# Context attention of a two-layer decoder: softmax division moved behind the weighted values, row sums by head-mask matmuls, the end of a row quantization on GpSimd

## The reference

```python
q = query @ Wq + bq;  kv = context @ Wkv + bkv          # 16 heads, head width 8
scores = einsum('bhid,bhjd->bhij', q, k) * 8 ** -0.5
scores = where(mask, -inf, scores)
attn = softmax(scores, axis=-1)
out = einsum('bhij,bhjd->bhid', attn, v)                 # heads side by side: 128 columns
x = x + out @ Wout + bout

def fp4_quant_dequant(x):                                # blocks of 16 along the row
    scale = max(max(abs(xb)) / 6, 1e-12)
    return grid(abs(xb / scale)) * sign(xb) * scale
gate = fp4_linear(layernorm(x), w_gate);  y = fp4_linear(layernorm(x), w_up)
x = x + fp4_linear(silu(gate) * y, w_down)
```

## Time and profile before

| | us |
|---|---|
| median of 3 runs (1272.89 to 1273.5) | 1272.97 |
| the profiled execution, its own time | 1272.73 |
| its span in the trace | 1270.8 |
| PE busy | 1128.9 (89%) |
| DVE busy | 901.9 (71%) |
| ACT busy | 879.7 (69%) |
| POOL busy | 627.9 (49%) |

### The profile page before, as it was taken

The page is one execution under the profiler, slowest core; times in us unless marked ns, Lnnn a source line. Parts: engine busy times, 40 slices in busy tenths (PEclk is TensorE's granted clock), DMA queues, the critical chain, the costliest instruction groups (busy, mean ns, idle before and its releaser), DMA issues.

```text
span 1270.8 us, 17038 instructions
## 1 busy us (share of the span) xinstructions
PE 1128.9 (89%) x6055; PEld 589.1 (46%) x6055; DVE 901.9 (71%) x1756; ACT 879.7 (69%) x1150; POOL 627.9 (49%) x463
## 2 busy tenths in 40 slices
PE   4899999999999999987888898799997999985765
PEld 2444444444444444432333332277775676653444
DVE  5766667766767677657888978546746786878885
ACT  2799999999989998992666767755564676733311
POOL 2577777777767777595455545013330300054232
PEclk9999999999999999996889989999998999997877
DMA  7200000000000000020000000000001000000000
GB/s 178 66 1 2 1 1 1 1 1 1 1 1 1 1 1 1 1 68 1 18 1 1 1 1 1 2 1 1 1 1 63 1 1 1 1 1 0 1 9 25
DMA packets 25631, 14.47 MB, mean 11 GB/s; under 512 B 14558, under 2 KB 24396, under 8 KB 25420
## 3 DMA queue, kind: packets, MB, share of 16 engines
q1 hardware_dynamic: 25548, 13.39, 3.7%
HBM read 12.34 MB, written 1.05 MB: 11 GB/s over the span
## 4 chain that ended last, share of the span: by engine, by line
PE 31%; POOL 31%; issue 20%; DVE 16%; ACT 1%; DMA 0%; POOLq 0%; SPq 0%; ACTq 0%; DVEq 0%
DVE ARENA L1159 6%; POOL ARENA L2711 6%; POOL ARENA L2709 6%; POOL ARENA L2705 6%; PE PS L1030 5%; POOL WQ L2722 3%; POOL ARENA L2735 3%; PE PS L900 3%; PE PS L1414 2%; PE PS L1004 2%; PE PS L832 2%; PE PS L1438 2%; PE PS L848 2%; PE PS L1405 2%; POOL WQ L2724 2%
## 5 line engine op out<-in xcount | busy, mean ns | idle before, releaser
L2565 DVE TENSOR_SCALAR ARENA<-PS,ARENA 128x512 f32<-128x512 f32 x256 | 174.5, 744 | 66.7 <-PE PS L2199 66.3
L1159 DVE TENSOR_REDUCE ARENA<-PS 128x1 f32<-128x512 f32 x256 | 160.9, 683 | 28.2 <-PE PS L848 27.7
L1075 ACT ACTIVATE ARENA<-PS 128x1024 f32<-128x1024 f32 x128 | 128.9, 1026 | 61.9 <-PE PS L886 61.6
L2378 ACT ACTIVATE ARENA<-ARENA 128x2048 f32<-128x2048 f32 x64 | 122.2, 1912 | 60.6 <-DVE ARENA L2565 60.1
L2199 PE MATMUL PS<-ARENA 64*128 64x512 f32 x512 | 129.0, 623 | 0.0
L2385 ACT ACTIVATE ARENA<-ARENA,consts_sb 128x2048 f32<-128x2048 f32 x64 | 124.6, 1994 | 0.4
L2209 PE MATMUL PS<-ARENA 128*64 128x512 f32 x512 | 118.7, 606 | 1.3 <-issue 1.3
L2391 ACT ACTIVATE ARENA<-ARENA 128x2048 f32<-128x2048 f32 x64 | 118.4, 1898 | 0.0
L2718 POOL TENSOR_SCALAR WQ<-ARENA,consts_sb 128x512 bf16<-128x512 f32 x32 | 22.3, 696 | 159.1 <-DVE ARENA L2541 159.1
L1340 POOL TENSOR_TENSOR ARENA<-ARENA 128x512 f32<-128x512 f32 x32 | 40.7, 1271 | 121.4 <-DVE ARENA L1298 120.9
L848 PE MATMUL PS<-ARENA 32*128 32x512 bf16 x256 | 74.0, 415 | 24.9 <-DVE ARENA L1159 19.8
(11 more groups left out here) (301 smaller groups left out, 2606.3 us busy)
## 6 DMA issues: line engine op xcount, KB each, us to landing
ARENA<-in_window_bias_dram SPq DMA_DIRECT2D x1, 1536.0 KB, 6.3
WKVG<-in_L_attn_W_in_dram SPq DMA_DIRECT2D x3, 448.0 KB, 5.6
X<-in_x_dram SPq DMA_DIRECT2D x4, 256.0 KB, 5.4
W<-in_L_ffn_w_dram SPq DMA_DIRECT2D x1, 1024.0 KB
out_dram<-X SPq DMA_DIRECT2D x4, 256.0 KB, 2.3
BV<-in_L_attn_b_in_dram SPq DMA_DIRECT2D x1, 512.0 KB, 6.7
Wout<-in_L_attn_W_out_dram SPq DMA_DIRECT2D x1, 512.0 KB, 4.7
WQ<-in_L_attn_wq_dram SPq DMA_DIRECT2D x1, 512.0 KB, 3.3
```

Source lines behind the costliest of these rows:

```text
L1075: act.activation(PT[m % PT_SLOTS], bank(("cP", m)), ACT.Exp, scale=0.5).then_inc(sem("c_exp"), 1)
L1159: dve.tensor_reduce(NMX[:, w % 2, t, h:h + 1], bank(("cS", n, j)), AX.X, ALU.max, negate=True).then_inc(sem("c_max"), 1)
L2378: act.activation(chunk(u, half), chunk(u, half), ACT.Sqrt).then_inc(sem("rooted"), 1)
L2565: dve.tensor_scalar(D[:, u % 2, kt, hd, :], bank(("S", u, c)), K2[:, u % 2, kt, hd:hd + 1], 1e-30, ALU.add, ALU.max).then_inc(sem("guarded ...
```

## The change

- The weights are no longer divided by their sum before they are transposed. sums and normalized go (DVE L1844 and L1845, POOL L1899, 16 times each), and the transposes wait for the exponential alone, one step earlier; ACT's copy turned also comes one step earlier.
- For each batch PE computes, behind the values (job eO), a second accumulation of four 128 x 512 matmuls of the same transposed weights with the head mask const("vhead") (job eZ): each output row holds the sum of its head. ACT inverts it as exp(-ln(sum)) (invert_sums), at t = 2 of the next batch, ahead of that step's exponential. DVE multiplies it with the values from PSUM into OTE (weighted, at the same step, ahead of quantize_y), in place of ACT's out_copy.
- project_out, turn_quantized and quantized_out move by a step or two; silu(0) stands behind invert_sums(3).
- quantize_y stops after seven of its nine instructions; the last two (a subtraction and the multiplication by the scales) are done by POOL, scaled_y, behind its subtraction of steps 11 and 15 (for batches 0 and 1), behind its stage E loop (batch 2), and behind step 2 of F (batch 3). hidden(1) and hidden(3) wait for them.
- SE has six buffers, not seven.

```diff
@@ tensor_e @@
                 for g in range(4):
                     mm = pe.matmul(o, VX[b][:, g, :], PTE[:, b % 2, g, :], start=g == 0, stop=g == 3)
                 done(mm, ("eO", b))
+                o = begin(("eZ", b))
+                heads = const("vhead").rearrange("p (g c) -> p g c", g=4)
+                for g in range(4):
+                    mm = pe.matmul(o, heads[:, g, :], PTE[:, b % 2, g, :], start=g == 0, stop=g == 3)
+                done(mm, ("eZ", b))
...
-            for s in range(STEPS + 2):
+            for s in range(STEPS + 1):
                 d_tail(s)
                 for n in scores_at(s):
                     scores(n)
-                if s < 2:
+                if s < 1:
                     continue
-                n = s - 2
+                n = s - 1
                 b, t = divmod(n, QT)
-                pe.wait_ge(sem("e_p"), n + 1)
+                pe.wait_ge(sem("e_exp"), n + 1)
...
                 if t == 0 and b:
                     values(b - 1)
-                if t == 1 and b:
+                if t == 2 and b:
                     project_out(b - 1)
-                if t == 0 and b >= 2:
+                if t == 3 and b >= 2:
                     turn_quantized(b - 2)
@@ scalar_e @@
-            def out_copy(b):
-                full(act, ("eO", b))
-                act.copy(OTE[:, b % 2], bank(("eO", b))).then_inc(sem("e_o"), 1)
-
-            for n in range(STEPS + 3):
+            def invert_sums(b):
+                full(act, ("eZ", b))
+                if b:
+                    act.wait_ge(sem("e_o"), b)
+                act.activation(ISUM, bank(("eZ", b)), ACT.Ln).then_inc(sem("e_sum"), 1)
+                act.wait_ge(sem("e_sum"), b + 1)
+                act.activation(ISUM, ISUM, ACT.Exp, scale=-1.0).then_inc(sem("e_isum"), 1)
+
+            for n in range(STEPS + 2):
                 b, t = divmod(n, QT)
                 d_tail(n)
                 if t == 1 and b >= 2:
                     rstd(5, b - 2)
+                if t == 2 and 1 <= b < B:
+                    invert_sums(b - 1)
                 if n < STEPS:
                     act.wait_ge(sem("e_shift"), n + 1)
-                    act.activation(SE[n % 7], SE[n % 7], ACT.Exp).then_inc(sem("e_exp"), 1)
-                if n == STEPS + 2:
-                    silu(act, 0)
-                if n >= 3:
-                    turned(n - 3)
-                if t == 3 and 1 <= b < B:
-                    out_copy(b - 1)
-                if t == 3 and b >= 2:
-                    quantized_out(act, b - 2)
-            out_copy(B - 1)
+                    act.activation(SE[n % 6], SE[n % 6], ACT.Exp).then_inc(sem("e_exp"), 1)
+                if n >= 2:
+                    turned(n - 2)
+                if t == 1 and b >= 3:
+                    quantized_out(act, b - 3)
+            invert_sums(B - 1)
+            silu(act, 0)
             quantized_out(act, B - 2)
@@ vector_e @@
-            def sums(n):
-                dve.wait_ge(sem("e_exp"), n + 1)
-                if n >= 3:
-                    dve.wait_ge(sem("e_p"), n - 2)
-                link(dve.tensor_reduce(SUE[:, n % 3], SE[n % 7], AX.X, ALU.add))
-                dve.reciprocal(RCE[:, n % 3], SUE[:, n % 3]).then_inc(sem("e_rc"), 1)
+            def weighted(b):
+                full(dve, ("eO", b))
+                dve.wait_ge(sem("e_isum"), b + 1)
+                if b >= 2:
+                    dve.wait_ge(sem("x_new"), 4 * B + b - 1)
+                dve.tensor_tensor(OTE[:, b % 2], ISUM, bank(("eO", b)), ALU.mult).then_inc(sem("e_o"), 1)
 
             for n in range(STEPS + 2):
                 b, t = divmod(n, QT)
                 if n < STEPS:
                     shift(n)
-                if n >= 2:
-                    sums(n - 2)
                 d_tail(n)
+                if t == 2 and 1 <= b < B:
+                    weighted(b - 1)
                 if b >= 2 and t == 0:
...
                 if b >= 2 and t == 2:
                     quantize_y(dve, link, b - 2)
+            weighted(B - 1)
             quantize_y(dve, link, B - 2)
             hidden(dve, link, 0, None)
@@ quantize_y, pool_e, hidden @@
-            quantize(dve, link, X_SCRATCH[1], P, Y[:, b].rearrange("p t d -> p (t d)"), S, YQ[:, b % 2].rearrange("p t d -> p (t d)"), "f_yq", last)
+            quantize(dve, link, X_SCRATCH[1], P, Y[:, b].rearrange("p t d -> p (t d)"), S, None, "y_added", last)
+
+        def scaled_y(pool, b):
+            scratch = X_SCRATCH[1]
+            rows = scratch[3][:, 0:S]
+            by = lambda t: t.rearrange("p (k i) -> p k i", i=BLK)
+            pool.wait_ge(sem("y_added"), b + 1)
+            pool.tensor_tensor(rows, rows, scratch[2][:, 0:S], ALU.subtract).then_inc(sem("y_rounded"), 1)
+            pool.wait_ge(sem("y_rounded"), b + 1)
+            if b >= 2:
+                full(pool, ("fX", b - 2))
+            scales = scratch[0][:, 1, 0:S // BLK].unsqueeze(2).to_broadcast([P, S // BLK, BLK])
+            pool.tensor_tensor(by(YQ[:, b % 2].rearrange("p t d -> p (t d)")), by(rows), scales, ALU.mult
+                               ).then_inc(sem("f_yq"), 1)
...
+                if n in (11, 15):
+                    scaled_y(pool, n // 4 - 2)
+            scaled_y(pool, B - 2)
             for n in range(STEPSF):
...
+                if n == 2:
+                    scaled_y(pool, B - 1)
...
+            if n in (1, 3):
+                dve.wait_ge(sem("f_yq"), B - 1 + n // 2)
```

More of the change, by code:

```diff
@@ L467, in d_tail, with values @@
         return []
+    def values(b, *pool):
+        return [(("eO", b), 1, [("e_o", b + 1)], *pool), (("eZ", b), 1, [("e_sum", b + 1)], *pool)]
     jobs = scores(0, "E3") + scores(1, "E3")
-    for s in range(steps + 2):
+    for s in range(steps + 1):
         jobs += d_tail(s)
@@ L473, in stage_e_jobs @@
             jobs += scores(n, pool_at(s))
-        if s >= 2:
-            b, t = divmod(s - 2, QT)
-            jobs += [(("eT", s - 2), 1, [("e_pt", s - 1)], pool_at(s))]
+        if s >= 1:
+            b, t = divmod(s - 1, QT)
+            jobs += [(("eT", s - 1), 1, [("e_pt", s)], pool_at(s))]
             if t == 0 and b:
-                jobs += [(("eO", b - 1), 1, [("e_o", b)], pool_at(s))]
-            if t == 1 and b:
+                jobs += values(b - 1, pool_at(s))
+            if t == 2 and b:
                 jobs += [(("eX", b - 1), 1, [("x_new", 4 * B + b)], pool_at(s))]
-            if t == 0 and b >= 2:
+            if t == 3 and b >= 2:
                 jobs += [(("fX", b - 2), 1, [("f_x", b - 1)], pool_at(s))]
-    jobs += [job + ("E4",) for job in gate_and_up_jobs(0)]
-    return jobs + [(("eO", B - 1), 1, [("e_o", B)], "E2"), (("eX", B - 1), 1, [("x_new", 5 * B)], "E2"),
-                   (("fX", B - 2), 1, [("f_x", B - 1)], "E2")]
+    jobs += [job + ("E4",) for job in gate_and_up_jobs(0)] + values(B - 1, "E2")
+    return jobs + [(("eX", B - 1), 1, [("x_new", 5 * B)], "E2"), (("fX", B - 2), 1, [("f_x", B - 1)], "E2")]
 def gate_and_up_jobs(n):
@@ L756, in decoder_kernel @@
         PTE, _ = carve(0, [2, 4, S])
-        SE = [carve(k, [HX, CK])[0] for k in (5376, 5888, 6400, 6912, 7424, 7936, 30848)]
+        SE = [carve(k, [HX, CK])[0] for k in (5376, 5888, 6400, 6912, 7424, 7936)]
         OTE, _ = carve(15872, [2, S])
@@ L1829, in shift @@
                 full(dve, ("eS", n))
-                if n >= 7:
-                    full(dve, ("eT", n - 7))
+                if n >= 6:
+                    full(dve, ("eT", n - 6))
                 if n >= 2:
                     dve.wait_ge(sem("e_shift"), n - 1)
-                dve.scalar_tensor_tensor(out=SE[n % 7], in0=bank(("eS", n)).rearrange("p (h j) -> p h j", h=HX),
+                dve.scalar_tensor_tensor(out=SE[n % 6], in0=bank(("eS", n)).rearrange("p (h j) -> p h j", h=HX),
                                          scalar=SCALEX, in1=MB[:, b].unsqueeze(1).to_broadcast([P, HX, CK]),
@@ L1896, in pool_e @@
                 add_bias(b)
-            def normalized(n):
-                pool.wait_ge(sem("e_rc"), n + 1)
-                pool.tensor_tensor(SE[n % 7], SE[n % 7], RCE[:, n % 3].unsqueeze(2).to_broadcast([P, HX, CK]),
-                                   ALU.mult).then_inc(sem("e_p"), 1)
-            for n in range(STEPS + 2):
-                if n < STEPS:
-                    pool.wait_ge(sem("e_max"), n + 1)
-                    pool.tensor_tensor(SE[n % 7], SE[n % 7], NME[:, n % 2].unsqueeze(2).to_broadcast([P, HX, CK]),
-                                       ALU.subtract).then_inc(sem("e_shift"), 1)
-                if n >= 2:
-                    normalized(n - 2)
+            for n in range(STEPS):
+                pool.wait_ge(sem("e_max"), n + 1)
+                pool.tensor_tensor(SE[n % 6], SE[n % 6], NME[:, n % 2].unsqueeze(2).to_broadcast([P, HX, CK]),
+                                   ALU.subtract).then_inc(sem("e_shift"), 1)
                 if n == ETAIL["weigh_end"]:
```

8 lines of the change are left out of this document (3 added, 5 removed).

## The result

| | before | changed |
|---|---|---|
| median, us | 1272.93 (1271.22 to 1273.5, 4 runs) | 1296.46 (1294.57 to 1297.67, 4 runs) |
| ratio, 95% interval | | 1.0188 (1.0172 to 1.0203), all of it above 1 |
| span of the profiled execution | 1270.8 | 1292.8 |
| its own time | 1272.73 | 1294.57 |

What follows compares the result with a forecast made beforehand. DVE was taken to bound stage E, but DVE and ACT would stand in order behind each pair and inversion: 1272.73 + 21.6 (stage E) + 0.9 (stage F) = 1295.2 us, forecast 1295, range 1284 to 1304.

Steps and rivals of the forecast that it cites:

- What bounds: Stage E: DVE is the bound, so work taken from it (net 16.7 us) counts unless a wait takes its place.
- Batch 0: Stage E, first batch: pair eO, eZ starts at 1130.6 us; shift(8) at 1145.9 against 1140.49, 5.4 us lost.
- Batch 1: Stage E, second batch: pair takes 9.4 us, DVE stands 10.3 us before weighted, shift(11) at 1169.7 us.
- Batch 2: Stage E, third batch: pair takes 8.7 us, DVE stands 11.2 us, shift(15) ends at 1195.2 against 1180.6 us.
- Batch 3: End of stage E: full-clock pair of 7.1 us, DVE stands 12.5 us, hidden(0) at 1216.2 against 1194.60 us.
- a wait of 10 to 12 us ahead of each of the last three weighted: Sign expected in the new trace: DVE waits this long before weighted in batches 1 to 3, released by ACT's Exp.
- Stage F: After stage E: quantize_y(3) shortens by 1.33 us but hidden(3) waits 2.2 us for POOL; +0.9, bounds -1.3 to +2.
- Full clock in all pairs: Rival for stage E's pairs: slower, but PE keeps full clock since it has more to do; 1289.4 us, chance 10%.
- The clock not coming back within a pair: Rival for stage E's pairs: low clock throughout, adding 2.5, 3.2 and up to 4.8 us; 1303 to 1306 us, chance 12%.
- Faster: Rival for stage E: the wait is hidden and DVE's 16.7 us less work counts; 1256 us, chance 6%.
- Half the price: Rival for stage E: PE and ACT run further ahead, each pair starts 2 to 3 us earlier; 1283 to 1287, chance 9%.
- Table loads: Rival for ACT's inversion: Ln and Exp need a table load each time, four or eight; 1300 to 1305 us, chance 3%.

Runs made afterwards that it cites:

- e2: Kernel before with only the last two instructions of quantize_y moved to POOL, softmax unchanged: 1271.36 us, ratio 0.9989.
- e1: Changed kernel with all nine instructions of quantize_y kept on DVE, so only the softmax half of the change: 1296.52 us, ratio 1.0183.
- e11: Kernel before with the end of quantize_y(0), (1) and (2) on POOL and quantize_y(3) wholly on DVE: 1272.03 us, ratio 1.0003.
- e4: Changed kernel, same instructions reordered: inversion, weighted and projection come later, quantize_y(2) ahead of weighted(3): 1281.47 us, ratio 1.0065.
- e5: e4 with eZ ahead of eO, silu(0) ahead of invert_sums(3) and hidden(0) ahead of weighted(3): 1279.06 us, ratio 1.0052.
- e6: e5 with eZ and eO split over two steps and the end of D one step earlier: 1277.9 us, ratio 1.0043.

## Why the prediction was right, step by step

- **What bounds.** DVE was the busiest engine of stage E, and its work fell by 17.6 us where 16.7 were summed. That DVE's work counts in full there is more than the runs show: in e2, 4.0 us less of it gave 1.6. The prediction's condition, unless a wait takes its place, held there as in the change. The loss came from waits, as the walk said. Two readings of the profile were off, neither in the sum: the longest of DVE's waits from 1105 us on isn't the 6.4 us for the end of D but one of 8.4 us, for TensorE's last down product (DVE X L2038 <- PE PS L1973: 9.2 us in three waits), at the very end of stage F; and the last of the 40 slices has DVE at 5 tenths, not at 7 or 8.
- **Batch 0.** shift(8) predicted 5.4 us later, measured 38.1 - 32.8 = 5.3. The pair started at 23.1 us from shift(0), predicted 22.9.
- **Batch 1.** The pair was priced at 9.4 us (clock lost once, for the first group) and took 1160.93 - 1150.98 = 9.95; the two halves were 6.67 and 3.60 us, as the rows of before had shown the loss to sit in the first group; the granted clock was 0.54 over the first half and 1.00 over the second. The stall was 10.7 us, predicted 10.3. The Trainium skill, "TensorE: Matmul & The Clock Gate", section "HAM oscillation — how this bites in real kernels", says that pauses make each round start at the low clock; in this batch the trace agrees (the first group 6.67 us against 3.70 at the full clock), in the next one it doesn't.
- **Batch 2.** Here a term was mis-sized. The pair began at 71.4 us, predicted 71.3, but ran at full clock from its start, 7.0 us where 8.7 were put:

```profile
1174.44 1.92 PE L1745 MATMUL PS<-W,ARENA 128*128 128x512 f32 x2
...
1176.14 1.06 PE L1782 MATMUL PS<-consts_sb,ARENA 128*128 128x128 f32 x4
...
1177.34 3.75 PE L1753 MATMUL PS<-ARENA,WKVG 128*128 128x512 f32 x8
...
1180.93 3.60 PE L1758 MATMUL PS<-ARENA,consts_sb 128*128 128x512 f32 x8
```

  The scores matmul and the transposes ahead of it (1.92 and 1.06 us, against 1.02 and 0.60 at full speed) still show the low clock, 0.54 granted from 1173.77 to 1177.34; over the pair's first group it was 0.98. So it rose before the pair, not within it. What differs from batch 1 is what PE did ahead of it: small work almost without a pause from 1173.77 on, while in batch 1 it had been idle for 3.06 us. That this is the cause isn't tested. The stall was 7.2 us instead of 11.2. A part of it only moved: normalize(5, 1) waited 2.8 us for its ACT pass, which stands in ACT behind the exponential that POOL's scaled_y(0) held back. The sum of both, 10.0, is nearer to the forecast than the row alone.
- **Batch 3.** From shift(15) to hidden(0) 24.1 us, predicted 22.3. The stall was 14.1 us, predicted 12.5. fX(1) and gate_and_up(0) ran at the low clock (1.11 us, and 4.65 us from its start to the pair's; granted 0.51), and a wait was overlooked: fG(0) takes the bank of fX(1) and starts only when ACT has copied it.

```profile
1195.04 1.11 PE L1737 MATMUL PS<-consts_sb,ARENA 128*128 128x128 f32 x4 [0.58 <-POOL ARENA L1894]
1196.19 0.59 ACT L1831 COPY ARENA<-PS 128x512 f32<-128x512 f32 x1 [1.03 <-PE PS L1737]
1196.92 4.81 PE L1983 MATMUL PS<-WKVG,ARENA 128*128 128x352 f32 x8 [0.77 <-ACT ARENA L1831]
1201.57 3.60 PE L1753 MATMUL PS<-ARENA,WKVG 128*128 128x512 f32 x8
1205.00 3.60 PE L1758 MATMUL PS<-ARENA,consts_sb 128*128 128x512 f32 x8
1208.63 0.60 ACT L1807 ACTIVATE ARENA<-PS 128x512 f32<-128x512 f32 x1 [11.86 <-PE PS L1758]
1209.26 0.63 ACT L1809 ACTIVATE ARENA<-ARENA 128x512 f32<-128x512 f32 x1
...
1209.98 0.69 DVE L1854 TENSOR_TENSOR ARENA<-ARENA,PS 128x512 f32<-128x512 f32 x1 [14.15 <-issue]
```

  This error of +1.8 and batch 2's of -2.0 nearly cancel: hidden(0) at 108.2, predicted 108.5. The forecast is thus a little better than its parts, which is luck. Of the signs it named, a wait of 10 to 12 us ahead of each of the last three weighted, only batch 1's is within the bounds (10.7, 7.2 and 14.1).
- **Stage F.** Predicted +0.9 us with bounds of -1.3 and +2, measured (168.8 - 108.2) - (145.1 - 86.9) = +2.4, outside them. In e1, without the POOL part, stage F is 0.4 us longer than before, so 2.0 of the 2.4 come with that part. hidden(3)'s wait was as said:

```profile
1242.51 1.26 POOL L1889 TENSOR_TENSOR ARENA<-ARENA 128x512 f32<-128x512 f32 x1 [2.28 <-DVE ARENA L1966]
1243.85 1.06 POOL L1894 TENSOR_TENSOR ARENA<-ARENA 128x512 f32<-128x512 f32 x1
1245.04 0.89 DVE L2047 TENSOR_TENSOR ARENA<-ARENA,PS 128x704 f32<-128x704 f32 x1 [2.61 <-POOL ARENA L1894]
```

  2.61 us less the 1.34 saved is +1.2 from hidden(2) to hidden(3). What I missed is the way from hidden(0) to hidden(1), 8.3 us against 7.3: gate_and_up(1) stands behind fX(2), which now waits for POOL, and takes 4.6 us at the low clock. e11 adds a caution: in the order of the kernel before, the hidden(3) wait costs nothing, because a later wait takes it up.
- **The rivals.** Full clock in all pairs: of the two pairs priced with a loss, one had none. The clock not coming back within a pair: in none. (Its first two terms, 2.5 and 3.2, make 1300.9 us of 1295.2; the 1303 to 1306 that it names need half or more of the last pair's 4.8.) Faster: refuted. Half the price: refuted, each stall began where the walk put it. Table loads: none beside the inversions in stage E; the one behind invert_sums(3) belongs to silu(0), as before. The Trainium skill's rule that ScalarE and VectorE keep strictly to their order ("TensorE: Matmul & The Clock Gate", section "Architectural detail: the array is 16x 32x32, not 1x 128x128") agrees with e4's trace, where quantize_y starts before the pair ends once the waiting instruction no longer stands ahead of it.
- **Where I went wrong was behind the prediction.** In e5 and e6 I took DVE waits off one by one and expected their sum. They were replaced by waits for TensorE; that had to be read from PE's busy time in the stretch, not from DVE's waits.

## What to carry to other kernels

Taking work off the busiest engine counts only if the engine isn't then made to wait in order: ask of every added wait when its releaser is started, and what stands behind it in the queue that could stand ahead. A result that takes 8 us to form should be awaited where its consumer would be that late anyway; moving the wait back, by a step in the first three batches and behind a quantization in the last, was worth 15 of 23.5 us here, with the same instructions. Once the order is mended, compare the busy times of the stretch again: the work given to TensorE (14 us in all) had made it the busiest engine, and three quarters of the part tested (7.8 of 10.6 us) came through to the end. Take such a stretch long enough to hold all of the moved work.

## What the runs showed of the hardware

The granted clock cost less than the pauses suggested: of the pairs behind long pauses, one lost 3.0 us in its first eight records (6.67 against 3.70 us), one lost nothing, as the clock had risen during the small work ahead of it (granted 0.54 from 1173.77 to 1177.34, then 0.98), and no second group of the changed kernel ran slow. And an ACT pass with Ln over 128 x 512 from PSUM took 0.60 us, 0.1 less than the nearest row I had priced it by (0.69 us, an activation with a bias column), so the inversion took 1.26 us from its first start to its end.

```profile
1138.84 0.60 ACT L1807 ACTIVATE ARENA<-PS 128x512 f32<-128x512 f32 x1
...
1139.47 0.63 ACT L1809 ACTIVATE ARENA<-ARENA 128x512 f32<-128x512 f32 x1
```

On POOL the two instructions of scaled_y aren't alike: the subtraction of two full 128 x 512 tiles took 1.26 us, the multiplication by the block scales 1.06 us (rows of stage F above). I had put 1.05 for both; this is 0.2 us of hidden(3)'s wait.
